# Decoder layer with attention, state-space scan and top-8 experts on one core: router sends split over the start of the expert stage, the last row's tail on other PSUM banks, and every queue's order written anew

## The chip, the core and the metric

One core of a Trainium2 chip runs one program. TensorE (PE in the profile, PEld for its weight loads) multiplies into PSUM banks; VectorE (DVE), ScalarE (ACT) and GpSimd (POOL) work element by element; SyncE (SP) only issues DMAs. POOL issues the indirect DMAs (gather and scatter by index). Each engine takes its instructions strictly in the order of its queue and waits at semaphores for the others. The metric is the device time of one execution in microseconds (us).

## The reference

```python
x = x + attn(layernorm(x))              # 4 rows of 512 tokens x 512; 16 heads of 128, one shared k and v
x = x + scan(ctx, layernorm(x))         # conv, 16 states: h = h * exp(dt*A) + dt*u*B ; y = sum(h*C)
x = x + moe(layernorm(x))               # 32 experts, the 8 best of each token, inner size 192
# moe: topv, topi = top_k(softmax(x @ gate.T), 8); weights under TAU are dropped, the rest renormed
```

## The kernel before

The four rows (index `b`, in the code also `r`) go one after the other, and a row's attention overlaps its scan and the end of the row before. The order of each engine's queue is written out call by call in the functions `first_row`, `row` (used three times) and `last_row`, once in each engine's block: SP from line 399, PE from 738, ACT from 1414, DVE from 2261, POOL from 2786.

**Start of row 0.** SP loads `Wq` (4 MB, into the tile `o_t`, line 366). `split_wq(g)` makes a high part of a quarter of it on ACT (line 1325) and a low part on DVE (line 2030), four quarters in `SPLIT_ORDER`. `first_stats`, `first_means`, `first_newton`, `first_norm` (lines 1969 to 1980) make the layer norm of x on DVE; `norm_tr` (PE, line 532) transposes it; `norm_hi`/`norm_lo` split the result. `scan_in` (PE, line 559) and `convolution` (DVE, lines 2021 and 2024, two pairs) feed the scan, `scan_u` (ACT) closes it, `scan_params` (line 585) and `step_size` (line 596) make its step. `keys_values`, `q_piece` (lines 573 to 575, 615 to 617), `key_squares`, `squares`, `q_scaled` (ACT) and `q_tr` lead to the first `scores`. `step_exp` and `step_log` (ACT, lines 1287 and 1294) belong to the scan's step.

**Scan.** For each of 16 states ACT makes `decays`, DVE `state_input`, two `state_scan` halves (line 2103) and `state_product`, and POOL adds the product to `y` by an accumulating DMA (`add_state`, line 2772). SP loads the b and c rows (`load_bc`, line 357).

**End of a row.** `out_proj(b, h)` (line 694) adds head h over four banks; it needs `load_wout(b, h)`, issued by SP in a written order among the `load_bc` (line 344). Then DVE: `last_sum`, `out_stats`, `out_means`, `out_gain`, `out_add`, `gate_stats`, `gated`, `add_scan`, `final_stats`, `final_norm`. The last row has no row behind it to overlap with. In it `proj_copy` (ACT) copies the projection from PSUM to SBUF ahead of `out_stats`; `out_tr` transposes the normed rows in four pieces, `out_copy` (ACT, line 1362) copies each to SBUF, `logits` (line 725) multiplies all four with the gate, and the router follows on DVE: `softmax_top`, `active`, then `ranks` on PE (lines 731 to 734), `slots` and `weights` (lines 2239 to 2244).

**Sends.** `send(t, k, ...)` scatters 128 tokens' entries to the list of the experts that they chose (line 2757): for each tile t of 128 tokens and each k, the k-th of a token's eight experts in ascending order of the expert. So the list of expert e is complete when the sends with k up to e have landed. A row has 32. Those of rows 0 to 2 are issued during the row behind (`send_some`); the 32 of row 3 stand at the head of the expert stage (`send_last`), four for each k.

**Expert stage.** 68 blocks of 128 tokens, two at least for each expert, in groups of four (`QUAD`). SP waits for the sends of expert e and loads the block's list (`get_ids`, lines 482 to 486); POOL gathers the tokens (`get`, line 2862); PE transposes, multiplies (lines 1145 and on), ACT weighs the result into `y_ring` (line 1894), and POOL adds it to the output by a scatter (`add`, line 2868). `get_next(q, r)` issues the gather for the block six further on. Before, POOL's order is: sends k = 0, 1; gets 0, 1; sends k = 2; gets 2, 3; sends k = 3; gets 4, 5; gets 6, 7; adds 0, 1; sends k = 4; gets 8, 9; adds 2, 3; sends k = 5; gets 10, 11; adds 4, 5; sends k = 6; gets 12, 13; adds 6, 7; sends k = 7; gets 14, 15; adds 8, 9; and from there gets and adds alone. Each get waits for the list that SP loads after the sends have landed.

## Time and profile before

| | us |
|---|---|
| median of 3 runs | 1616.96 |
| their range | 1614.8 to 1628.02 |
| the profiled execution | 1621.45 |
| its span on the core | 1619.7 |

PE is busy 86% of the span, DVE 69%, ACT 58%, POOL 30%. The mean granted clock of TensorE is 0.936 of full speed. In the 40 slices of the span PE is at 9 tenths nearly throughout, except in the first three slices, in slices 28 to 31 (about 1134 to 1296 us: the last row's tail and the start of the expert stage), where it shows 4, 3, 6, 5, and in the neighbours of these. Rows 0 to 3 take some 1145 us, the tail and the router 70, and the expert stage 405.

### The profile page before, as it was taken

The page shows a single profiled execution, that of the slowest core. Times are in us where ns is not written, and L with a number is a line of the kernel's source. Part 1 is how long each engine was busy: PE and PEld are TensorE (multiplying, and loading weights), DVE is VectorE, ACT ScalarE, POOL GpSimd, SP SyncE. Part 2 cuts the span into 40 slices and gives each one's busy share as a digit, 9 for nine tenths or more (in the row PEclk, how much of TensorE's full clock was granted, in tenths as well). Part 3 has the DMA queues.
Part 4 walks back from the last instruction along what each step waited for, and adds up shares of the span by engine and source line. Part 5 has one row for each costly group of instructions (what it writes and reads, how often), then busy time and mean ns, then how long its engine had stood idle before and what let it go on. Part 6 is the DMA issues. An engine that isn't in the chain of part 4 may idle for free.

```text
span 1619.7 us, 26021 instructions
## 1 busy us (share of the span) xinstructions
PE 1394.1 (86%) x6762; PEld 999.7 (62%) x6763; DVE 1110.4 (69%) x1547; ACT 944.5 (58%) x2428; POOL 486.6 (30%) x367
## 2 busy tenths in 40 slices
PE   4899898999999899999899999898436548999996
PEld 1577665548887455887644678763225436777774
DVE  5365598858898786878886887786853326666662
ACT  4667684468878246877725687763213325666652
POOL 0000010000143502006250210206426446666663
PEclk9799999999999999999999999999757779999998
DMA  6538987623679742576973267578124449999985
GB/s 240 201 109 223 292 204 178 151 93 81 182 193 227 179 107 80 126 230 138 226 175 94 61 173 208 116 175 250 41 87 104 102 98 222 223 238 231 243 185 67
DMA packets 137435, 265.44 MB, mean 164 GB/s; under 512 B 45944, under 2 KB 47433, under 8 KB 128512
## 3 DMA queue, kind: packets, MB, share of 16 engines
q0 software_dynamic: 36480, 126.75, 35.0%
q1 hardware_dynamic: 75120, 86.70, 18.5%
q10 hardware_dynamic: 25744, 50.87, 10.0%
...
## 4 chain that ended last, share of the span: by engine, by line
PE 50%; DMA 18%; issue 10%; DVE 9%; ACT 5%; SPq 3%; POOL 2%; POOLq 1%; ACTq 1%; DVEq 0%
PE bank L694 13%; PE bank L671 8%; DMA out<-y_ring,add_ids 4%; PE bank L654 4%; DMA y<-state 4%; PE pair L615 3%; PE pair L616 3%; PE pair L617 3%; DMA wout<-in_wout 2%; PE bank L532 2%; DMA c_bc<-bc_dram 2%; DMA y<-dbu 2%; PE pair L532 2%; PE pair L559 2%; DVE dbu L2103 1%
## 5 line engine op out<-in xcount | busy, mean ns | idle before, releaser
L694 PE MATMUL bank<-wout,o_t 128*128 128x512 f32 x512 | 241.0, 627 | 27.4 <-DMA wout<-in_wout 16.3
L671 PE MATMUL bank<-v_aug,probs 128*128 128x129 f32 x2048 | 249.1, 277 | 10.1 <-ACT probs L1331 7.1
L671 PEld LDWEIGHTS bank<-v_aug,probs 128*128 128x128 f32 x2048 | 240.5, 192 | 27.4 <-ACT probs L1331 19.9
L2757 POOL DMA_INDIRECT lists<-entry,slot x128 | 197.6, 1543 | 83.4 <-DVE entry L2244 44.7
L694 PEld LDWEIGHTS bank<-wout,o_t 128*128 128x128 f32 x512 | 101.2, 201 | 154.8 <-issue 154.3
L1331 ACT ACTIVATE probs<-bank 128x512 f32<-128x512 f32 x256 | 152.2, 604 | 69.0 <-PE bank L654 31.8
L1340 ACT ACTIVATE decay<-delta,neg_a 128x511 f32<-128x511 f32 x256 | 164.4, 725 | 24.4 <-DVE state L2103 12.1
L2868 POOL DMA_INDIRECT out<-y_ring,add_ids x68 | 125.0, 1838 | 96.6 <-DMA out<-y_ring,add_ids 52.3
L2772 POOL DMA_DIRECT2D y<-dbu x32 | 29.2, 913 | 412.6 <-DVE dbu L2108 254.0
L2103 DVE TENSOR_TENSOR_SCAN state<-decay,state 128x1024 f32<-128x1024 f32 x64 | 144.8, 2281 | 6.5 <-ACT decay L1340 4.7
L2103 DVE TENSOR_TENSOR_SCAN dbu<-decay,dbu 128x1024 f32<-128x1024 f32 x64 | 144.7, 2279 | 5.1 <-ACT decay L1340 4.2
L654 PE MATMUL bank<-q_t,k_t 128*128 128x512 f32 x256 | 126.8, 607 | 1.7 <-ACT q_t L1320 1.4
L615 PE MATMUL pair<-wq,xn_hi 128*128 128x512 f32 x256 | 110.2, 431 | 2.2 <-ACT q_s L1310 2.0
L2753 POOL DMA_DIRECT2D wq<-wq_dram x30 | 22.0, 765 | 300.1 <-PE pair L617 226.3
L1145 PE MATMUL bank<-w_hi,xt_hi 128*128 x272 | 99.9, 367 | 9.7 <-DVE xt_lo L2697 8.0
L1348 ACT ACTIVATE o_s<-bank,den 128x128 f32<-128x128 f32 x256 | 80.1, 373 | 46.4 <-DVE den L2121 41.1
...
L2862 POOL DMA_INDIRECT x_blk<-xf_dram,get_ids x70 | 85.2, 1218 | 60.9 <-DMA get_ids<-lists 31.8
L616 PE MATMUL pair<-wq,xn_hi 128*128 128x512 f32 x256 | 101.8, 398 | 0.0
L617 PE MATMUL pair<-wq,xn_lo 128*128 128x512 f32 x256 | 101.6, 397 | 0.0
L1881 ACT ACTIVATE xt_hi<-pair (+1 forms) x70 | 41.9, 598 | 102.1 <-PE pair L532 95.0
...
## 6 DMA issues: line engine op xcount, KB each, us to landing
...
```

The costliest lines, as they stand in the source:

```text
L615: pe.matmul(bank_q[t % 2][:], xn_hi[:, k, tile], wq[:, 0, k, :], start=(k == 0), stop=False)
L616: pe.matmul(bank_q[t % 2][:], xn_hi[:, k, tile], wq[:, 1, k, :], start=False, stop=False)
L617: mm = pe.matmul(bank_q[t % 2][:], xn_lo[:, k, tile], wq[:, 0, k, :], start=False, stop=(k == KT - 1))
L654: mm = pe.matmul(bank_s[k % 2][:], k_t[:, tile], q_t[:, j, :], start=True, stop=True)
L671: mm = pe.matmul(bank_o[half][:, (t % 2) * (DH + 1):(t % 2 + 1) * (DH + 1)], probs[:, k, t * P:(t + 1) * P], v_aug[:, k, :], start=(k == 0 ...
L694: mm = pe.matmul((bank_o + bank_s)[t][:], o_t[:, h, t * P:(t + 1) * P], wout[:, h % 4, :], start=(h == 0), stop=(h == H - 1))
L1145: pe.matmul(gu_bank[:, 0:2 * INTER], xt_hi[:, parity, k, :], hi[:, k, :], start=(k == 0), stop=False)
L1331: act.activation(probs[:, k, :], bank_s[k % 2][:], ACT.Exp).then_inc(S["exp_ok"], 1)
L1340: act.activation(dA3[:, e, 1:], delta[:, e, 1:], ACT.Exp, scale=neg_a[:, bass.ds(n, 1), e:e + 1].rearrange("p a c -> p (a c)")).then_inc(S ...
L2103: dve.tensor_tensor_scan(now, dA3[:, es, :].rearrange("p e t -> p (e t)"), now, 0.0, ALU.mult, ALU.add).then_inc(S["scan_ok"], 1)
L2757: pool.indirect_dma_start(out=lists, out_offset=bass.IndirectOffsetOnAxis(ap=slot[:, t, k:k + 1].bitcast(U32), axis=0), in_=entry[:, t, :] ...
L2868: pool.indirect_dma_start(out=out, out_offset=bass.IndirectOffsetOnAxis(ap=add_ids[:, r:r + 1].bitcast(U32), axis=0), in_=y_ring[:, r, :], ...
```

## The change

There are three parts.

1. **Sends of row 3.** POOL's new order is: sends k = 0, 1, 2; gets 0, 1; sends k = 3; gets 2, 3; sends k = 4; gets 4, 5; sends k = 5; gets 6, 7; adds 0, 1; sends k = 6; gets 8, 9; adds 2, 3; sends k = 7; gets 10, 11; adds 4, 5; and from there gets and adds alone. Each get of block pair e then stands behind sends up to k = e + 2.
2. **Tail of the last row.** `proj_copy` is gone there: `out_stats` and `out_gain` read the PSUM banks of the projection. The transposes of the scan's y use `bank_q`, those of the normed rows four banks of their own with no wait. `out_copy` is shared, ACT k = 0 and 2, DVE k = 1 and 3, and the gate's product is made piece by piece (`logit_part`). `weights` stands ahead of `slots`, `tokens` ahead of `gate_norm`, and the loads of experts 0 to 3 stand later in ACT's queue.
3. **Orders.** In all rows the calls on SP, PE, ACT, DVE and POOL are in a new order. In row 0, DVE begins with `split_wq` of the first quarter, ahead of `first_stats`, and has three quarters of it ahead of the second `convolution`; ACT has `split_wkv` and two `split_wq` ahead of `first_seed`, and `step_exp`, `step_log` ahead of `q_seed`, which it takes after `key_squares` and two `squares`.

The diff, cut: row 0's start on PE, ACT and DVE, the tail, SP's and POOL's last row, and the sends. The rows between are reordered in the same manner.

```diff
...
-y_banks = lambda b: bank_s if b == NB - 1 else bank_t[0:1]
-f_banks = lambda b: bank_o if b == NB - 1 else bank_t[0:1]
+y_banks = lambda b: bank_q if b == NB - 1 else bank_t[0:1]
+f_banks = lambda b: bank_o + bank_t if b == NB - 1 else bank_t[0:1]
...
-    if k >= len(banks):
-        pe.wait_ge(S["fT_ok"], b * KT + (k + 1 - len(banks)))
+    if b < NB - 1 and k > 0:
+        pe.wait_ge(S["fT_ok"], b * KT + k)
...
+def logit_part(b, k):
+    if k % 2 == 0:
+        pe.wait_ge(S["fT_ok"], b * KT + k // 2 + 1)
+    else:
+        pe.wait_ge(S["fTd_ok"], k // 2 + 1)
+    for t in range(TT):
+        mm = pe.matmul(bank_s[0][:, t * NE:(t + 1) * NE], end_s[:, k, t * P:(t + 1) * P], w_gate[:, k, :], start=(k == 0 and t == 0),
+                       stop=(k == KT - 1 and t == TT - 1))
+    if k == KT - 1:
+        mm.then_inc(S["lg_ps"], 1)
...
     scan_in(0, 2)
+    norm_tr(0, 0)
     scan_in(0, 3)
-    norm_tr(0, 0)
     norm_tr(0, 1)
+    norm_tr(0, 2)
     scan_params(0)
-    norm_tr(0, 2)
     norm_tr(0, 3)
     step_size(0, 0)
+    keys_values(0, 0)
     step_size(0, 1)
-    keys_values(0, 0)
+    keys_values(0, 1)
     step_size(0, 2)
+    keys_values(0, 2)
     step_size(0, 3)
-    keys_values(0, 1)
-    keys_values(0, 2)
     q_piece(0, 0, 0)
+    q_piece(0, 0, 1)
     keys_values(0, 3)
-    q_piece(0, 0, 1)
...
     neg_rates()
+    scan_pad(0, 0)
+    split_wkv()
+    split_wq(SPLIT_ORDER[0])
+    split_wq(SPLIT_ORDER[1])
+    scan_pad(0, 1)
     first_seed(0)
-    scan_pad(0, 0)
-    scan_pad(0, 1)
     scan_pad(0, 2)
-    split_wkv()
+    norm_hi(0, 0)
+    split_wq(SPLIT_ORDER[2])
     scan_pad(0, 3)
+    norm_hi(0, 1)
     scan_u(0)
-    norm_hi(0, 0)
-    norm_hi(0, 1)
-    split_wq(SPLIT_ORDER[0])
+    scan_rows(0)
     norm_hi(0, 2)
     norm_hi(0, 3)
-    scan_rows(0)
-    split_wq(SPLIT_ORDER[1])
     step_parts(0, 0)
     step_parts(0, 1)
-    split_wq(SPLIT_ORDER[2])
+    split_wq(SPLIT_ORDER[3])
     step_parts(0, 2)
     step_parts(0, 3)
     value_copy(0, 0)
-    step_exp(0)
-    step_log(0)
     key_squares(0)
-    value_copy(0, 1)
     squares(0, 0, 0)
     squares(0, 0, 1)
+    step_exp(0)
     q_seed(0, "q0")
+    step_log(0)
...
-    load_expert(0)
     divide(b, 15, 1)
     split_expert(0, 0)
-    load_expert(1)
+    decays(b, 11)
+    head_copy(b, 14)
     decays(b, 12)
-    split_expert(0, 1)
-    head_copy(b, 14)
-    split_expert(1, 0)
-    head_copy(b, 15)
     decays(b, 13)
     decays(b, 14)
-    load_expert(2)
+    load_expert(1)
+    split_expert(0, 1)
+    split_expert(1, 0)
     decays(b, 15)
-    proj_copy(b, 0)
-    proj_copy(b, 1)
-    proj_copy(b, 2)
-    proj_copy(b, 3)
+    head_copy(b, 15)
     norm_seed(b, "o")
     norm_seed(b, "z")
     gates(b)
+    load_expert(2)
     norm_seed(b, "f")
+    load_expert(3)
+    out_copy(b, 0)
     split_expert(1, 1)
+    out_copy(b, 2)
+    logit_exps(b)
     split_expert(2, 0)
-    out_copy(b, 0)
-    out_copy(b, 1)
-    out_copy(b, 2)
-    out_copy(b, 3)
     split_expert(2, 1)
-    logit_exps(b)
-    load_expert(3)
...
+def proj_out(b, t):
+    return (bank_o + bank_s)[t][:] if b == NB - 1 else o_c[:, t, :]
 def out_stats(b, t):
-    dve.wait_ge(S["oc_ok"], b * TT + t + 1)
-    stats(b, "o", o_c[:, t, :], t)
+    if b == NB - 1:
+        dve.wait_ge(S["op_ps"], b * TT + t + 1)
+    else:
+        dve.wait_ge(S["oc_ok"], b * TT + t + 1)
+    stats(b, "o", proj_out(b, t), t)
...
-    dve.tensor_tensor(x_sb[:, t, :], x_sb[:, t, :], (bank_s[t % 2] if b == NB - 1 else bank_t[0])[:], ALU.add).then_inc(S["x2_ok"], 1)
+    dve.tensor_tensor(x_sb[:, t, :], x_sb[:, t, :], (bank_q[t % 2] if b == NB - 1 else bank_t[0])[:], ALU.add).then_inc(S["x2_ok"], 1)
...
+def out_copy(b, k):
+    dve.wait_ge(S["fT_ps"], b * KT + k + 1)
+    dve.tensor_copy(end_s[:, k, :], (bank_o + bank_t)[k][:]).then_inc(S["fTd_ok"], 1)
...
 def first_row():
+    split_wq(SPLIT_ORDER[0])
     first_stats(0, 0)
     first_stats(0, 1)
     dve.wait_ge(S["w_in_sb"], 16 * N_W)
...
     first_norm(0, 0)
     first_norm(0, 1)
     convolution(0, 0)
-    convolution(0, 1)
     first_norm(0, 2)
+    split_wq(SPLIT_ORDER[1])
     first_norm(0, 3)
+    split_wkv()
     norm_lo(0, 0)
     norm_lo(0, 1)
-    split_wkv()
-    split_wq(SPLIT_ORDER[0])
+    split_wq(SPLIT_ORDER[2])
+    convolution(0, 1)
     norm_lo(0, 2)
     norm_lo(0, 3)
-    split_wq(SPLIT_ORDER[1])
-    split_wq(SPLIT_ORDER[2])
+    softplus(0)
     q_norm(0, "k")
     q_norm(0, "q0")
     keys(0, 0)
+    softplus_rest(0)
+    split_wq(SPLIT_ORDER[3])
     keys(0, 1)
-    split_wq(SPLIT_ORDER[3])
+    key_lo(0)
     q_norm(0, "q1")
-    softplus(0)
-    key_lo(0)
-    softplus_rest(0)
+    softplus_log(0)
+    denominators(0, 0, 0)
+    denominators(0, 0, 1)
+    denominators(0, 1, 0)
+    q_lows(0, 0, 2)
+    softplus_sum(0)
+    scan_du(0)
     wq_stored(dve)
     skip(0)
-    q_lows(0, 0, 2)
...
...
     load_bc(b, 9)
     load_bc(b, 10)
     load_bc(b, 11)
+    load_wout(b, 4)
+    load_wout(b, 5)
     load_bc(b, 12)
-    load_wout(b, 5)
-    load_wout(b, 4)
+    load_wout(b, 7)
     load_wout(b, 6)
     load_bc(b, 13)
-    load_wout(b, 7)
     load_wout(b, 8)
+    load_wout(b, 10)
+    load_bc(b, 14)
     load_wout(b, 9)
-    load_bc(b, 14)
+    load_wout(b, 11)
+    load_bc(b, 15)
+    load_wout(b, 14)
     load_wout(b, 12)
-    load_wout(b, 10)
-    load_bc(b, 15)
     load_wout(b, 13)
-    load_wout(b, 11)
-    load_wout(b, 14)
     load_wout(b, 15)
...
     last_sum(b)
+    out_stats(b, 0)
     dve.wait_ge(S["oT_ok"], NB * H)
     split(0, 0)
-    out_stats(b, 0)
     out_stats(b, 1)
...
+    tokens(b)
     gate_norm(b)
     split(0, 1)
...
+    out_copy(b, 1)
+    out_copy(b, 3)
     split(1, 0)
     softmax_top(b)
     active(b)
+    weights(b)
     slots(b)
-    weights(b)
     split(1, 1)
...
 def last_row(b):
+    add_state(b, 5)
     send_some(b - 1, 0, 3)
-    add_state(b, 5)
     add_state(b, 6)
     send_some(b - 1, 3, 6)
+    send_some(b - 1, 6, 9)
     add_state(b, 7)
     add_state(b, 8)
     add_state(b, 9)
+    send_some(b - 1, 9, 12)
+    send_some(b - 1, 12, 15)
     add_state(b, 10)
     add_state(b, 11)
-    send_some(b - 1, 6, 9)
+    send_some(b - 1, 15, 18)
     add_state(b, 12)
-    send_some(b - 1, 9, 12)
-    send_some(b - 1, 12, 15)
     add_state(b, 13)
-    send_some(b - 1, 15, 18)
     send_some(b - 1, 18, 21)
     add_state(b, 14)
...
-send_last(range(0, 2))
+send_last(range(0, 3))
 pool.wait_ge(S["xf_out"], NB * 16)
 pool.wait_ge(S["blank_ok"], 1)
 pool.wait_ge(S["rows_ok"], 2)
-for r in range(2):
+for r in range(QUAD):
+    if r % MIN_BLK == 0 and r > 0:
+        send_last(range(r // MIN_BLK + 2, r // MIN_BLK + 3))
     pool.wait_ge(S[f"get_in{r}"], 32)
     get(r)
-send_last(range(2, 3))
-for r in range(2, QUAD):
-    pool.wait_ge(S[f"get_in{r}"], 32)
-    get(r)
-send_last(range(3, 4))
+send_last(range(4, 5))
 for r in range(2):
     get_next(-1, r + 2)
 last_quad = pool.value_load(tab[0:1, T_LAST:T_LAST + 1], min_val=NE * MIN_BLK // QUAD - 1, max_val=MAX_BLK // QUAD - 1)
 pool.wait_ge(S["x2_out"], NB * 16)
 for q in range(2):
     for r in range(0, QUAD, 2):
-        k = q * 2 + r // 2 + 3
-        if k in range(4, TOPK):
+        k = q * 2 + r // 2 + 5
+        if k < TOPK:
             send_last(range(k, k + 1))
         get_next(q, r)
         get_next(q, r + 1)
         add_pair(q, r)
-send_last(range(TOPK - 1, TOPK))
```

## Rows read from the trace of the kernel before

**Rows 1.** Windows: stretch, us, busy of PE PEld DVE ACT POOL, clock, DMA share, GB/s.
```profile
120.00:200.00 80.00, 71.14 (x398) 56.23 (x397) 42.33 (x37) 53.94 (x166) 5.03 (x6) 0.96 0.93 260
200.00:300.00 100.00, 88.31 (x433) 59.63 (x432) 85.23 (x72) 57.12 (x140) 9.06 (x11) 0.97 0.77 187
435.00:770.00 335.00, 321.29 (x1656) 232.16 (x1655) 272.57 (x368) 229.33 (x673) 105.65 (x76) 0.98 0.63 161
1215.00:1345.00 130.00, 77.78 (x345) 62.36 (x345) 44.19 (x86) 42.22 (x72) 66.60 (x53) 0.78 0.48 109
1345.00:1608.00 263.00, 241.96 (x1229) 190.10 (x1227) 164.71 (x317) 152.48 (x262) 166.76 (x108) 0.99 0.86 207
```
**Rows 2.** Timeline, ACT's weighed blocks 7 and 13: start, us, engine line op [idle before].
```profile
1292.41 0.69 ACT L1894 ACTIVATE y_ring<-bank,meta 128x512 f32 x1 [2.03 <-PE bank L1164]
1346.17 0.69 ACT L1894 ACTIVATE y_ring<-bank,meta 128x512 f32 x1 [0.96 <-PE bank L1164]
```
**Rows 3.** The line view of L1894: count, duration min/median/max in ns, first and last start.
```profile
L1894 ACT ACTIVATE y_ring<-bank,meta x68: 687/688/692, 1238.7 to 1607.8; 128x512 f32 x68
```
**Rows 4.** Timeline, POOL at the start of the expert stage.
```profile
1201.93 1.67 POOL L2757 DMA_INDIRECT lists<-entry,slot  x1 [44.71 <-DVE entry L2244]
...
1218.40 1.05 POOL L2862 DMA_INDIRECT x_blk<-xf_dram,get_ids  x1 [5.82 <-DMA get_ids<-lists]
...
1250.23 1.03 POOL L2757 DMA_INDIRECT lists<-entry,slot  x1 [0.31 <-issue]
...
1260.43 2.29 POOL L2862 DMA_INDIRECT x_blk<-xf_dram,get_ids  x1 [4.77 <-DMA get_ids<-lists]
...
1287.52 1.03 POOL L2862 DMA_INDIRECT x_blk<-xf_dram,get_ids  x1 [1.71 <-DMA get_ids<-lists]
1289.36 1.62 POOL L2868 DMA_INDIRECT out<-y_ring,add_ids  x1 [0.81 <-issue]
...
1328.02 1.05 POOL L2862 DMA_INDIRECT x_blk<-xf_dram,get_ids  x1 [7.61 <-issue]
```
**Rows 5.** DMA issues: out<-in, queue, KB each, median us from issue to landing.
```profile
o_t<-in_wq SPq DMA_DIRECT2D x1, 4096.0 KB, 14.5
```
**Rows 6.** Timeline, start of row 0, in order of time, all engines.
```profile
11.77 0.51 SPq L366 DMA_DIRECT2D o_t<-in_wq  x1
14.85 1.29 DVE L1969 BATCH_NORM_STATS2 st<-q_s 128x6 f32<-128x512 f32 x2
20.96 4.06 DVE L2024 SCALAR_TENSOR_TENSOR dbu<-decay,conv_w,dbu 128x512 f32<-128x512 f32 x6
30.75 1.97 PE L532 MATMUL pair<-const,probs 128*128 128x128 f32 x8 [7.49 <-DVE probs L1980]
32.65 4.61 PE L585 MATMUL bank<-state,w_x 128*48 128x512 f32 x8
33.34 1.90 ACT L1325 ACTIVATE du<-o_t 128x2048 fp32r<-128x2048 f32 x1
35.28 2.29 DVE L2030 TENSOR_TENSOR o_t<-o_t,du 128x2048 fp32r<-128x2048 f32 x1
40.16 2.46 PE L596 MATMUL pair<-x_dbl,w_dt 16*128 16x512 f32 x4 [1.88 <-DVE xn_lo L2039]
77.28 1.97 PE L532 MATMUL pair<-const,q_s 128*128 128x128 f32 x8 [4.56 <-ACT q_s L1310]
```
**Rows 7.** Timeline, the last row's projection and closing sum.
```profile
1126.03 22.97 PE L694 MATMUL bank<-wout,o_t 128*128 128x512 f32 x48 [5.51 <-DMA wout<-in_wout]
1146.21 2.29 DVE L2115 TENSOR_TENSOR o_t<-y,state 128x2048 f32<-128x2048 f32 x1 [2.28 <-PE bank L694]
```
**Rows 8.** Timeline, the tail: transposes, gate product, first instruction of `weights`.
```profile
1177.22 3.90 PE L532 MATMUL bank<-const,xf 128*128 128x128 f32 x16 [5.80 <-DVE xf L1980]
1181.86 4.27 PE L725 MATMUL bank<-w_gate,o_t 128*128 128x32 f32 x32 [0.75 <-ACT o_t L1362]
...
1199.72 0.29 DVE L2239 TENSOR_TENSOR o_t<-o_t 128x128 f32<-128x128 f32 x1
```

614 lines of the change are left out of this document (305 added, 309 removed).

## The prediction

> **What bounds the kernel now.** I read the page first, then windows over each stage, then the timelines of the places that the diff touches. The windows show three regimes. In the rows PE sets the pace: in 335 us of the middle it is busy 321.3 and idle 13.7, with DVE at 272.6 [rows 1]. The late blocks of the expert stage are bound by PE as well (242 of 263 us) [rows 1]. Between them lies a stretch, 1215 to 1345 us, where PE is busy 78 of 130 us and DVE and ACT a third of the time [rows 1]. There POOL's queue sets the pace. The weighed blocks show it: the first is at 1238.7, block 13 at 1346.17, the last (67) at 1607.8 [rows 2, 3]. So the first 13 take 107.5 us, 8.3 each, and the other 54 take 261.6 us, 4.84 each. At the start, row 0 isn't bound by PE: it waits for norms, conversions and the scan's step.
>
> **Sends (part 1).** Before, the gets of blocks 8 and 14 start at 1260.43 and 1328.02 [rows 4]: three pairs in 67.6 us, 22.5 a pair. In each pair the queue is four sends (from 1250.23 to 1260.43 less the idle of 4.77, so to 1255.66: 5.4; up to 0.8 more where one is slow), then the wait until these sends have landed and SP has loaded the list from them (4.77 and, three pairs on, 7.61), the gets with another wait of about 2 between them (1.71 in the row), and two adds of 1.6 each with gaps of 0.3 to 0.8 [rows 4]. PE follows the gather four blocks ahead: block 7 is weighed at 1292.41, 4.9 after the get of block 11 at 1287.52 [rows 2, 4].
>
> After, a get finds its sends two pairs old, so both waits go. A pair is then 5.6 of sends, 2.75 of two gets, 3.8 of two adds and 0.9 of gaps, some 13. The four more sends ahead of get 0 cost nothing: eight sends run from 1201.93 at about 1.29 each to 1212.6, the next four end at 1217.9, and get 0 starts at 1218.40 since it waits 5.82 for its list [rows 4]. The adds of blocks 0 and 1 ended just before 1250.23 [rows 4]. After, sends k = 4 and 5 stand ahead of them besides; that is eight sends more than before, of which four fit in the gap of 5.8 and one is offset by other short waits in that stretch: +4 x 1.29 less these, so this point comes at some 1252 (1255 without the offset, within the bounds below). From there: sends k = 6 to 1257.6; get 8 at 1259.7, with 2 us kept for blocks whose result is late; gets and adds and sends k = 7, get 10 at 1272.6; get 11 at 1275.3, so block 7 at 1275.3 + 4.9 = 1280.2. No send is left behind it, and six blocks at PE's own 4.84 put block 13 at 1309.2, against 1346.17: **-37** for the likely case. Bounds: with pairs of 11 to 12 us (no slow send) the gain is 41. From above, if each of the first pairs keeps one wait of 4.77, two pairs lose 9.5, and the pace of 4.84 begins one pair later (6 us lost at most against it): -37 + 9.5 + 4 = about -24.
>
> **Tail (part 2).** The transposes of the normed rows start at 1177.22 and the gate product ends at 1186.13, with four copies on ACT between [rows 8]. Four banks and copies on two engines close the gap of 0.75 and let the pieces of the product (4.27 in all) run behind each copy; but PE's own work, 3.90 + 4.27, stays, of 8.91 in all: -0.7 to -1, I take -1.0. `weights` (five small instructions, from 1199.72 [rows 8], sends from 1201.93 [rows 4]: 1.4 us of DVE) goes under the ranks, which PE makes while DVE waits: -1.4. `tokens` now waits for row 2's sends ahead of `gate_norm`; POOL's last one ended 44.71 before 1201.93, at 1157.2 [rows 4], and the new place comes at about 1161, so the wait is covered by 3 to 4 us; without that cover it would cost at most those. Sum: **-2.4**, from 0 to -4. The removed `proj_copy` is worth nothing by itself: `last_sum` (1146.21, 2.29) runs on DVE at the same time [rows 7], and DVE makes the same four statistics behind it, now from PSUM. If a read from PSUM made each of the eight `out_stats` and `out_gain` 0.1 us longer, that would be +0.8; I keep it in the range and not in the sum.
>
> **End of the last row (part 3).** PE stalls 5.51 us ahead of 1126.03 for a `wout` load [rows 7]: The written order issues head 12's ahead of head 10's. The new order has 10 ahead of 14 and 12, and each load but one stands at or ahead of its old place. The stall would go, -5.5; but some of the time is taken by the closing sum, which waits for the scan's last add, with POOL's sends in front. I take **-5**, from -8 to 0.
>
> **Rows 0 to 2 (part 3).** The same amount of work in another order, on PE, which idles only 14 us in 335 [rows 1]. All of that gone would be -14 in each row, one more stall like that of the last row 5.5 and a colder clock behind it. Neither can be read from a queue order, so I take **0**, and keep +23 (a stall of 7.6 in each) as a rival.
>
> **Start of row 0 (part 3), against the change.** `Wq` is issued at 11.77 [rows 6] and takes 14.5 us to land [rows 5]: 26.3. Before, DVE starts its statistics at 14.85 and has both convolutions done by 29.7, in the shadow of this load; PE has the first norm transpose at 30.75, the scan's product at 32.65, `step_size` at 40.16 and the first `q_tr` at 77.28 [rows 6]. After, the first thing in DVE's queue is the low part of a quarter of `Wq`, which waits for the load and for ACT's high part (1.90): 26.3 + 1.9 + 2.29 = 30.5 [rows 5, 6]. Only then statistics (2.6 for four tiles), aggregation and the seed from ACT (some 2), two norms (1.0), the first convolution (4.06 + 0.9 for its first products), a norm, a quarter of `Wq` (2.2), a norm: the first norms are transposed at about 44 instead of 30.75. The second convolution stands behind two `norm_lo`, `split_wkv` (1.2) and a third quarter (2.3): done at about 58. Then `scan_u`, `scan_params` (4.61) and the first `step_size` at about 65.8 instead of 40.16: +25.6. ACT adds `step_exp` and `step_log` ahead of the seed for q; each works on 128x2048 like the conversions (1.90), but needs all four `step_size`; and `key_squares` waits for all keys. That makes another 3.8 and the four `step_size` between keys: the first `q_tr` comes at about 111 instead of 77.28, **+33**. Of this PE can give back what it idles later in the row: 80.0 - 71.1 and 100.0 - 88.3 [rows 1], 8.9 + 11.7 = 20.6. So the front is +13 at least, and +39 if ACT's extra pieces line up badly. I take +33, since the scan on DVE starts as late as the heads and its chain then lies on the end of the row.
>
> The Trainium skill speaks against it as well: "DMA: Bandwidth & Descriptors", section "Rules for kernel authors", says to issue a DMA early, do compute, and wait on its semaphore late; here DVE waits first and computes behind it. Its section "Anatomy of one DMA — SWDGE (gpsimd) path" gives about 2.0 us and bytes over 436 GB/s, that is an estimate of 11.6 us for 4 MiB where the row has 14.5 [rows 5]; by it the front would cost 2.9 less.
>
> **Sum.** -37 - 2.4 - 5 + 0 + 33 = -11.4. The profiled execution took 1621.45 (span 1619.7), 4.5 above the median of 1616.96; so 1610.0 for it, and 1605.5 as the median.
>
> **The rivals.**
> - *The front is absorbed.* PE and DVE fill their idle time in row 0 and take back 20: 1605.5 - 20 = 1585.5. For it: the idle time is there, and the heads don't depend on the scan until the row's end. Against: that idle time has its own reasons (DMA share 0.93 in 120 to 200 [rows 1]). Chance 0.26.
> - *Slower.* The new orders of SP put a `wout` load behind b and c loads in each of rows 0 to 2, and PE stalls 5.5 and runs colder for 2.1 in each: +22.8, and the last row keeps its 5: 1605.5 + 22.8 + 5 = about 1633. It decides from one and a half stalls a row on. Against: the middle rows' orders differ by a few places only. Chance 0.12.
> - *A new wait on the sends' way.* The adds, the gathers and the loads of lists crowd, and pairs stay near 18 us: -24 instead of -37, 1605.5 + 13 = 1618.5. For it: a single get waited 7.61 for a list though one pair before 4.77 sufficed [rows 4]. Chance 0.14.
> - The forecast: 1605.5, its own range 1596 to 1614. Chance 0.48.
>
> **How the numbers follow.** A measurement of this kernel tells 1% (16 us) from no change: faster is below 1600.8, slower above 1633.1. Faster is the first rival and a fifth of the forecast's case: 0.36. Slower: the second, 0.12. Same: the rest, 0.52. The range for 8 in 10 goes from 1580 (below it a third of the absorbed case) to 1630 (above it the slow one).
>
> **What would show it.** Right: the first norm transpose on PE near 44 and the first `q_tr` near 111; no waits of 4 us or more for lists ahead of gets 8 to 15, and block 13 weighed some 70 us behind the first block instead of 107.5; no gap of 5 us in the last row's projection. Wrong: a row 0 whose PE idle behind the late start is well under 20 us (the first rival); a PE idle in rows 0 to 2 well over 14 us in 335 (the second); pairs of gets still 18 us or more apart (the third).

## The result, and the profile after

| | before | after |
|---|---|---|
| median of 20 runs | 1617.2 | 1623.45 |
| lowest | 1604.65 | 1618.88 |
| ratio after/before, 95% interval | | 1.0046 (1.0025 to 1.0067) |
| span of the profiled execution | 1619.7 | 1623.6 |

The change is 0.46% slower, about 7 us. Forecast was 11 us faster. One of the 20 executions after took 2371.56 us, at a mean granted clock of 0.553, and is left out of the ratio. The time lies within the range and within 1% of before, but on the other side.

In the following table both traces are cut at the same places, from the start of one kind of instruction to the next. It accounts for 2.7 of the 3.9 us between the two spans; the other 1.2 lie behind block 67.

| stretch | before | after | difference | forecast |
|---|---|---|---|---|
| start to the first exps of row 0 | 81.3 | 117.5 | +36.2 | +33 |
| first exps of row 0 to those of row 1 | 281.7 | 290.3 | +8.6 | 0 |
| row 1 to row 2 | 273.5 | 279.9 | +6.4 | 0 |
| row 2 to row 3 | 275.3 | 277.6 | +2.3 | 0 |
| row 3, first to last exps | 167.9 | 162.1 | -5.8 | -5, with the next |
| last exps to the end of the projection | 69.3 | 73.3 | +4.0 | |
| end of the projection to the first send of row 3 | 52.9 | 47.1 | -5.9 | -2.4 |
| first send to block 0 weighed | 36.7 | 34.2 | -2.5 | 0 |
| block 0 to block 13 | 107.5 | 74.6 | -33.0 | -37 |
| block 13 to block 67 | 261.6 | 254.0 | -7.6 | 0 |
| sum | | | +2.7 | -11.4 |

The forecast's two large terms are there. Three rows behind them were forecast at 0 and cost 17.

**Expert stage.** Windows of the kernel after: stretch, us, busy of PE PEld DVE ACT POOL, clock, DMA share, GB/s. They answer to [rows 1]:

```profile
120.00:200.00 80.00, 71.28 (x391) 56.00 (x391) 46.78 (x45) 52.77 (x165) 4.12 (x5) 0.97 0.43 110
200.00:300.00 100.00, 92.09 (x546) 72.65 (x545) 77.06 (x70) 74.03 (x214) 9.37 (x12) 0.97 0.96 261
...
1260.00:1345.00 85.00, 61.63 (x296) 49.41 (x297) 36.31 (x72) 35.78 (x61) 59.92 (x50) 0.85 0.59 136
1345.00:1610.00 265.00, 249.51 (x1277) 197.57 (x1276) 171.99 (x331) 158.73 (x272) 171.24 (x111) 1.00 0.89 215
```

These windows (one left out, 435 to 770 us) don't hold the same blocks as those of [rows 1]: before, block 13 is weighed at the end of the stretch from 1215 to 1345, and here 11 us behind its end. From the first get to block 13, the same work in both kernels (first line before, second after):

```profile
1218.40:1346.20 127.80, 78.97 (x350) 63.09 (x351) 44.91 (x87) 42.46 (x73) 67.67 (x53) 0.78 0.49 114
1265.10:1356.50 91.40, 72.31 (x349) 57.33 (x349) 44.56 (x87) 42.47 (x73) 65.81 (x51) 0.89 0.66 155
```

It takes 91.4 us instead of 127.8, and PE is busy 79% of it instead of 62%. Of the 36 us, 6.7 are PE's busy time itself: it does the same work at a mean granted clock of 0.89 instead of 0.78. The last stretch is denser too: PE is busy 94% of it where it was 92%. The blocks, by the timeline and the line view of ACT's y_ring (they answer to [rows 2, 3]):

```profile
1328.75 0.69 ACT L1903 ACTIVATE y_ring<-bank,meta 128x512 f32 x1 [2.03 <-PE bank L1179]
1356.46 0.69 ACT L1903 ACTIVATE y_ring<-bank,meta 128x512 f32 x1 [0.99 <-PE bank L1179]
L1903 ACT ACTIVATE y_ring<-bank,meta x68: 687/688/691, 1281.9 to 1610.5; 128x512 f32 x68
```

Blocks 0, 7, 13 and 67 are weighed at 1281.9, 1328.75, 1356.46 and 1610.5. POOL's timeline shows the pairs (they answer to [rows 4]); the gets are L2884, sends L2779, adds L2890:

```profile
1265.11 1.05 POOL L2884 DMA_INDIRECT x_blk<-xf_dram,get_ids  x1 [0.80 <-issue]
...
1303.29 1.05 POOL L2884 DMA_INDIRECT x_blk<-xf_dram,get_ids  x1 [0.31 <-issue]
...
1305.98 2.20 POOL L2890 DMA_INDIRECT out<-y_ring,add_ids  x1 [0.30 <-issue]
1312.59 1.56 POOL L2890 DMA_INDIRECT out<-y_ring,add_ids  x1 [4.41 <-DMA out<-y_ring,add_ids]
...
1321.32 1.06 POOL L2884 DMA_INDIRECT x_blk<-xf_dram,get_ids  x1 [0.30 <-issue]
...
1327.82 1.08 POOL L2884 DMA_INDIRECT x_blk<-xf_dram,get_ids  x1 [0.30 <-issue]
```

No get waits more than 0.82 us for its list any more: get 8 at 1303.29 stands 0.31 behind its predecessor, where it had waited 4.77 [rows 4]. Gets 8, 10 and 12 come 18.0 and 6.5 us apart. In the first of these gaps one add waits 4.41 for an earlier add; up to get 12 this is the one wait of over 1 us that is left. One pair, 8 to 10, is thus as slow as the prediction's third rival had it.

POOL's waits (line waited for: us in total, times, longest), before from 1200 to 1345 us and then after from 1240 to 1350:

```profile
POOL x_blk L2862 <- DMA get_ids<-lists: 31.8, 8, 7.9
```

```profile
POOL x_blk L2884 <- DMA get_ids<-lists: 1.1, 2, 0.8
```

**Start of row 0.** Timeline of the kernel after, in order of time (it answers to [rows 6]):

```profile
25.91 1.91 ACT L1340 ACTIVATE du<-o_t 128x2048 fp32r<-128x2048 f32 x1 [5.97 <-DMA o_t<-in_wq]
27.93 2.29 DVE L2039 TENSOR_TENSOR o_t<-o_t,du 128x2048 fp32r<-128x2048 f32 x1 [26.94 <-ACT du L1340]
30.13 1.28 DVE L1978 BATCH_NORM_STATS2 st<-q_s 128x6 f32<-128x512 f32 x2
43.19 1.12 PE L532 MATMUL pair<-const,probs 128*128 128x128 f32 x4 [21.21 <-DVE probs L1989]
52.81 4.06 DVE L2033 SCALAR_TENSOR_TENSOR dbu<-decay,conv_w,dbu 128x512 f32<-128x512 f32 x6
66.75 2.04 PE L596 MATMUL pair<-x_dbl,w_dt 16*128 16x512 f32 x2 [2.20 <-DVE xn_lo L2048]
113.47 1.12 PE L532 MATMUL pair<-const,q_s 128*128 128x128 f32 x4 [5.53 <-ACT q_s L1325]
```

DVE waits 26.94 us for ACT's first half, which waits for `Wq`. The statistics start at 30.13; before, the first two of the four tiles stood at 6.30, ahead of the 14.85 that the prediction reads as their start [rows 6], and the other two at 14.85. Behind them the first norm transpose comes at 43.19 instead of 30.75, the first `step_size` at 66.75 instead of 40.16, the first `q_tr` at 113.47 instead of 77.28.

**Last row and tail.** Timeline of PE in the kernel after (it answers to [rows 7, 8]):

```profile
1156.18 10.54 PE L694 MATMUL bank<-wout,o_t 128*128 128x512 f32 x24 [2.46 <-DMA wout<-in_wout]
1169.71 13.56 PE L694 MATMUL bank<-wout,o_t 128*128 128x512 f32 x24 [2.99 <-DMA wout<-in_wout]
1183.80 3.67 PE L694 MATMUL bank<-wout,o_t 128*128 128x512 f32 x8 [0.52 <-DMA wout<-in_wout]
1189.65 3.67 PE L694 MATMUL bank<-wout,o_t 128*128 128x512 f32 x8 [2.18 <-DMA wout<-in_wout]
...
1226.82 3.67 PE L532 MATMUL bank<-const,xf 128*128 128x128 f32 x16 [6.15 <-DVE xf L1989]
1230.29 3.76 PE L735 MATMUL bank<-w_gate,o_t 128*128 128x32 f32 x32
```

The stall of 5.51 in one piece became four of 2.46, 2.99, 0.52 and 2.18, 8.15 in all. In the tail the gap between transposes and gate product is gone, and both together take 7.2 us instead of 8.9.

**Rows 1 to 3.** PE's waits from 270 to 1160 us: the kernel before (with its stall of 5.5 in the last projection), then after (with the first of the four above).

```profile
PE bank L694 <- DMA wout<-in_wout: 16.3, 7, 5.5
PE bank L694 <- issue: 8.3, 3, 3.5
```

```profile
PE pair L532 <- DVE probs L1989: 16.1, 3, 6.0
PE bank L694 <- DMA wout<-in_wout: 13.5, 4, 3.8
PE bank L694 <- issue: 4.2, 4, 1.1
```

A wait that wasn't there stands first: three times some 5.4 us, once in each row, PE's `norm_tr` waits for DVE's `first_norm` (line 1989). `norm_tr(r, 0)` waits for all four of them (line 540), so for the last. The middle one of the three, first DVE, then PE:

```profile
584.41 2.29 DVE L2104 TENSOR_TENSOR dbu<-du,b_bc 128x2048 f32<-128x2048 f32 x1 [5.31 <-DMA c_bc<-bc_dram]
...
592.77 2.28 DVE L2112 TENSOR_TENSOR_SCAN dbu<-decay,dbu 128x1024 f32<-128x1024 f32 x1
594.97 0.52 DVE L1989 TENSOR_SCALAR probs<-q_s,mv,rs_n 128x512 f32<-128x512 f32 x1
...
595.55 1.12 PE L532 MATMUL pair<-const,probs 128*128 128x128 f32 x4 [4.84 <-DVE probs L1989]
```

DVE itself stands still for 5.31 us ahead of `state_input` 12 (line 2104), which comes before all four norms, for that state's b and c rows. In the three rows DVE waits 5.66, 5.31 and 6.49 us there, and PE 5.20, 4.84 and 6.03. In the kernel before DVE has no such wait, and the fourth norm is done 4.6, 4.1 and 3.1 us before PE comes for it.

The three rows as a whole, from the first exps of row 0 to those of row 3 (windows; before, then after):

```profile
81.30:911.80 830.50, 782.33 (x3809) 542.80 (x3808) 633.11 (x735) 539.46 (x1541) 170.20 (x133) 0.97 0.63 163
117.50:965.30 847.80, 791.52 (x3821) 545.97 (x3821) 631.02 (x740) 536.80 (x1543) 173.84 (x133) 0.96 0.61 158
```

Of the 17.3 us only 8.1 are idle time of PE (56.3 instead of 48.2; other waits have shrunk beside the new 16.1). The other 9.2 are busy time: the granted clock is 0.96 instead of 0.97, and 12 more matmuls fall into the stretch, nearly all of them in row 0. Seven are missing from row 3's heads in exchange (964 instead of 971), so part of the +8.6 and of the -5.8 in the first table is work that has changed its stretch.

### The profile page after: what moved, and what is told of

It reads as the page before. It is cut to its first block, busy times and chain, and to the rows that moved or that the text cites. A ratio compares the mean times of both kernels' runs of the same rounds, so it can differ in the third digit from the quotient of the medians.

```text
span 1623.6 us, 26011 instructions
## 1 busy us (share of the span) xinstructions
PE 1393.9 (86%) x6762; PEld 993.7 (61%) x6763; DVE 1108.8 (68%) x1549; ACT 936.9 (58%) x2422; POOL 493.5 (30%) x367
## 4 chain that ended last, share of the span: by engine, by line
PE 42%; DMA 27%; DVE 12%; issue 10%; ACT 5%; POOL 2%; SPq 2%; POOLq 1%; DVEq 0%; ACTq 0%
DMA out<-y_ring,add_ids 14%; PE bank L671 10%; PE bank L694 7%; PE bank L654 5%; DMA y<-state 3%; DMA wout<-in_wout 3%; DMA y<-dbu 3%; PE pair L615 2%; PE pair L617 2%; PE pair L616 2%; DMA c_bc<-bc_dram 2%; PE bank L532 2%; PE pair L532 2%; DVE dbu L2033 1%; DVE state L2117 1%
## 5 line engine op out<-in xcount | busy, mean ns | idle before, releaser
L694 PE MATMUL bank<-wout,o_t 128*128 128x512 f32 x512 | 248.1, 641 | 23.5 <-DMA wout<-in_wout 19.2
L671 PEld LDWEIGHTS bank<-v_aug,probs 128*128 128x128 f32 x2048 | 239.8, 192 | 23.9 <-ACT probs L1346 18.4
L2779 POOL DMA_INDIRECT lists<-entry,slot x128 | 205.1, 1603 | 100.3 <-DVE slot L2275 61.2
L2890 POOL DMA_INDIRECT out<-y_ring,add_ids x68 | 125.1, 1840 | 92.2 <-DMA out<-y_ring,add_ids 71.1
L615 PE MATMUL pair<-wq,xn_hi 128*128 128x512 f32 x256 | 110.9, 433 | 15.6 <-ACT q_s L1325 10.9
L2104 DVE TENSOR_TENSOR dbu<-du,b_bc 128x2048 f32<-128x2048 f32 x32 | 73.2, 2289 | 41.6 <-DMA c_bc<-bc_dram 26.9
L1363 ACT ACTIVATE o_s<-bank,den 128x128 f32<-128x128 f32 x256 | 80.7, 380 | 34.5 <-DVE den L2130 27.4
L1161 PE MATMUL bank<-w_lo,xt_hi 128*128 x272 | 92.6, 340 | 0.0
L1162 PE MATMUL bank<-w_hi,xt_lo 128*128 x272 | 92.3, 340 | 0.0
```

The costliest lines, as they stand in the source:

```text
L615: pe.matmul(bank_q[t % 2][:], xn_hi[:, k, tile], wq[:, 0, k, :], start=(k == 0), stop=False)
L671: mm = pe.matmul(bank_o[half][:, (t % 2) * (DH + 1):(t % 2 + 1) * (DH + 1)], probs[:, k, t * P:(t + 1) * P], v_aug[:, k, :], start=(k == 0 ...
L694: mm = pe.matmul((bank_o + bank_s)[t][:], o_t[:, h, t * P:(t + 1) * P], wout[:, h % 4, :], start=(h == 0), stop=(h == H - 1))
L2779: pool.indirect_dma_start(out=lists, out_offset=bass.IndirectOffsetOnAxis(ap=slot[:, t, k:k + 1].bitcast(U32), axis=0), in_=entry[:, t, :] ...
L2890: pool.indirect_dma_start(out=out, out_offset=bass.IndirectOffsetOnAxis(ap=add_ids[:, r:r + 1].bitcast(U32), axis=0), in_=y_ring[:, r, :], ...
```

## The experiments

Each ratio is to the kernel before, timed beside it. The medians of that kernel went from 1612.74 to 1621.17 in these four sets, so the ratios are compared and not the medians. "Changed" is the kernel after. The five kernels for the start of row 0 have one execution each; for those the trace is read.

### The large terms: front_old, sends_only, old_orders, rows_old

Whole functions are exchanged between the two kernels.

```diff
 # front_old = changed, but on all five queues:
-first_row() of after
+first_row() of before
 # rows_old = changed, but on all five queues:
-row(b, r) of after
+row(b, r) of before
 # sends_only = before, and on POOL behind last_row:
-send_last(range(0, 2)) ... send_last(range(TOPK - 1, TOPK))   # before
+send_last(range(0, 3)) ... k = q * 2 + r // 2 + 5             # after
 # old_orders = changed with first_row and row of before, and last_row of before up to last_sum,
 #              then the new tail
```

> The changed kernel with the first_row of the kernel before on all five queues. My theory (the late start of row 0 costs 36 us and nothing gives it back): the first exps at 81 instead of 117.5, all behind it earlier by 36, so 1623.5 - 36 = 1587, ratio to the kernel before 0.982. Rival (row 0 and the rows behind absorb most of it): less than 15 us, 1608 or more, ratio over 0.994.

> The kernel before with only the new order of row 3's sends. My theory (POOL's sends and the waits for lists pace the first 13 blocks): block 13 weighed some 70 to 75 us behind the first one instead of 107.5, and the whole kernel 33 to 40 us faster, 1577 to 1584, ratio 0.976 to 0.980. Rival (much of the gain in the changed kernel comes from the tail or from where the loads of experts stand): under 25 us, ratio over 0.985.

> The kernel before with the new sends and the new tail behind last_sum, and every queue's old order up to there. My theory (the new orders are where the gain goes): sends -33 to -40, tail -2 to -8, so -35 to -48: 1569 to 1582, ratio 0.970 to 0.978. Rival (the tail needs the new order of the last row): no better than the sends alone.

> The changed kernel with the row function of the kernel before on all five queues, so rows 0 to 2 behind their start. From single traces the scores of row 1 lag by 37 us and those of row 3 by 45. Theory 1 (the new order of the rows costs these 8 us): 1615.5, ratio to the kernel before 0.999. Theory 2 (the 8 us are scatter from run to run): 1623.5, ratio 1.004.

| | median | ratio to before (95%) |
|---|---|---|
| front_old | 1582.31 | 0.978 (0.972 to 0.984) |
| sends_only | 1578.97 | 0.976 (0.970 to 0.982) |
| old_orders | 1574.98 | 0.977 (0.970 to 0.983) |
| rows_old | 1610.87 | 0.996 (0.993 to 1.000) |

*front_old*: the start of row 0 costs the changed kernel its 36 us in the end as well (1.0046 - 0.978, 2.7%, 43 us with an uncertainty of 10). Nothing behind gives it back. *sends_only*: the sends are worth 2.4% by themselves. Its blocks 0, 13 and 67 are weighed 72.5 and 252.5 us apart. *old_orders*: with the new tail besides, 0.977, it is no better than the sends alone, as the rival had it, but two ratios with 0.6% of uncertainty each can't show the tail; tail_only below does. *rows_old*: the new order of the rows costs; with the old one the changed kernel is 0.8% (13 us, with an uncertainty of 7) faster. In its trace the rows from exps to exps take 283.7, 273.5 and 274.0 instead of 290.3, 279.9 and 277.6. So it wasn't scatter.

### Where row 0 loses: seed_early, conv_pair, seed_conv, seed_conv_exp, seed_conv_keys

All are edits of the changed kernel's first_row; the later ones contain the earlier.

```diff
 # seed_early; DVE:
-split_wq(SPLIT_ORDER[0])        # first in the queue
...
 convolution(0, 0)
+split_wq(SPLIT_ORDER[0])
 # ACT: first_seed(0) behind neg_rates(), scan_pad(0, 1) behind scan_pad(0, 0)
 # conv_pair; DVE: convolution(0, 1) right behind convolution(0, 0); ACT: scan_pad(0, 2), (0, 3), scan_u(0)
 #            ahead of norm_hi(0, 0); PE: norm_tr(0, 0) behind scan_in(0, 3)
 # seed_conv = both
 # seed_conv_exp; ACT:
+step_exp(0)
+step_log(0)
 key_squares(0)
...
-step_exp(0)
 q_seed(0, "q0")
-step_log(0)
 # seed_conv_keys; PE: step_size(0, 0), (0, 1), keys_values(0, 0), step_size(0, 2), (0, 3),
 #                 keys_values(0, 1), (0, 2), q_piece(0, 0, 0), keys_values(0, 3), q_piece(0, 0, 1)
```

> The changed kernel; in row 0 alone, DVE's low part of the first quarter of Wq moved from the head of its queue to behind the first convolution, and ACT's first_seed and second scan_pad ahead of its two conversions. Theory 1 (the wait for Wq at the head of two queues is the main cause of the 36 us): the first norm transpose on PE at about 31 instead of 43.2 and the first exps 25 to 33 us earlier, 85 to 92. Theory 2 (mine: two delays of like size in series, the wait for Wq and the second convolution behind three conversions): norm transpose at 31, but the first exps only about 11 us earlier, 106.

> The changed kernel; in row 0 alone, the second convolution right behind the first on DVE, with scan_pad, scan_u and scan_in moved forward on ACT and PE so that it can. Theory 1: the first exps hardly earlier, under 5 us. Theory 2: the first step_size at about 55 instead of 66.8, the first exps about 11 us earlier, 106.

> Both edits of row 0 together. Theory 2: step_size near 43, and the first exps at about 92, that is 25 us earlier than in the changed kernel; the 10 us that stay against the 81.3 of the kernel before are those of step_exp, step_log and key_squares on ACT. If it is still over 100, a third delay in the new order of row 0 is larger than I hold it to be.

> The two edits of row 0 (seed_conv) and, besides, ACT's step_exp and step_log ahead of key_squares, where ACT idles 6.5 us for the last keys. The third delay by my theory: these two (1.90 each) and DVE's softplus behind them hold up the q norms by 5 us. Expected: first exps at 91 to 92 instead of 96.0. Rival (the late fourth keys_values holds everything up): 96.

> seed_conv_exp with, besides, PE's order of step_size, keys_values and q_piece at the start of row 0 as before: four step_size nearly together, and the last keys_values ahead of the second q_piece. Theory 1 (PE's interleaving of these is the third delay): the first exps at 87 to 89 instead of 96.3. Rival (the order of ACT and DVE behind them keeps it): 94 to 96.

Measured, each in one trace:

| | first norm_tr | first step_size | first q_tr | first exps | time |
|---|---|---|---|---|---|
| before | 30.75 | 40.16 | 77.28 | 81.3 | |
| after | 43.19 | 66.75 | 113.47 | 117.5 | |
| seed_early | 33.88 | 57.67 | 106.90 | 110.9 | 1617.73 |
| conv_pair | 49.22 | 61.68 | 104.24 | 108.3 | 1615.84 |
| seed_conv | 34.88 | 46.56 | 91.97 | 96.0 | 1601.13 |
| seed_conv_exp | 35.40 | 47.22 | 92.26 | 96.3 | 1596.53 |
| seed_conv_keys | 35.61 | 47.62 | 85.79 | 89.8 | 1596.96 |

Theory 1 of seed_early fell: with the wait for `Wq` out of the way the first exps come only 6.6 us earlier. The convolution alone gives 9.2, both 21.5. Theory 2 had 11, 11 and 25. Simple delays in series would give 15.8 together; 5.7 come only when both are gone, so each alone is partly hidden behind the other (conv_pair's first `norm_tr` even comes 6.0 later than after). The single values carry some scatter: over all traces with the whole new start the first exps stand at 117.5 to 122.7, over those with the whole old one at 75.1 to 83.2. seed_conv_exp changed nothing, so my reason for the third delay was wrong. The trace of seed_conv_exp showed another: PE's four `step_size` stand apart by a `keys_values` each, and the last `keys_values` behind two `q_piece`. ACT's key_squares waits for it, and q waits for ACT:

```profile
72.03 0.28 ACT L1281 ACTIVATE junk<-bank 128x128 bf16<-128x128 f32 x1 [4.09 <-PE bank L575]
78.02 0.76 PE L615 MATMUL pair<-wq,xn_hi 128*128 128x512 f32 x1 [6.03 <-ACT q_s L1325]
```

The first is ACT, idle 4.09 until the last `keys_values` (line 575), the second PE, idle 6.03 until ACT has scaled q. With PE's old order (seed_conv_keys) the first `q_piece` of the second pair starts at 71.36 instead of 78.02, and the exps at 89.8, 6.5 us earlier:

```profile
71.36 0.77 PE L615 MATMUL pair<-wq,xn_hi 128*128 128x512 f32 x1 [3.63 <-ACT q_s L1325]
```

The gap is larger than scatter where it arises: from the first `step_size` to the first `q_tr` it is 38.2 us instead of 45.0. Its one execution doesn't show these 6.5 (1596.96 beside 1596.53), but the kernel before had a median of 1621.17 beside the one and of 1612.74 beside the other. Whether they last to the end was not settled. Some 8 us of the 36 are left in orders that weren't tried one by one.

### Why the rows are longer: norm_tr_late, norms_early, sp_rows_old

```diff
 # norm_tr_late; PE, row:
-norm_tr(r, 0)
 out_proj(b, 4)
-norm_tr(r, 1)
-norm_tr(r, 2)
 out_proj(b, 5)
+norm_tr(r, 0)
+norm_tr(r, 1)
+norm_tr(r, 2)
 norm_tr(r, 3)
 # norms_early; DVE, row:
 first_means(r)
+first_newton(r)
 state_scan(b, 11, 1)
+first_norm(r, 0)
+first_norm(r, 1)
 state_input(b, 12)
 state_product(b, 11)
-first_newton(r)
 state_scan(b, 12, 0)
-first_norm(r, 0)
-first_norm(r, 1)
 # sp_rows_old = changed with row of before on SP alone
```

> The changed kernel; in the rows, PE's four norm_tr of the next row moved behind out_proj(b, 5), nothing else. The trace of the changed kernel shows PE idle 16.1 us in three stays before norm_tr, waiting for DVE's first_norm. Theory 1 (this wait is what makes the new rows slower): -10 to -16 us, 1608 to 1613, ratio to the kernel before 0.994 to 0.998. Theory 2 (the wait moves on to the next product, which waits for a wout load or for the same norms): under 4 us, ratio 1.002 or more.

> The changed kernel; in the rows, DVE's first_newton and the first two first_norm moved ahead of state_input 12, state_product 11 and the first half of state_scan 12 (6.9 us of DVE), as in the kernel before; nothing else. Theory 1 (DVE's late norms make the new rows 4.4 us longer each, 278.7 instead of 274.3): the wait of 5.4 before norm_tr goes without coming back, 8 to 13 us faster than the changed kernel, 1610 to 1615, ratio to the kernel before 0.996 to 0.999. Theory 2 (PE's later waits, for wout and for norm_lo, take its place, as when norm_tr was moved): under 4 us, ratio 1.002 or more.

> The changed kernel with SP's order of the rows as before, every other queue new. Theory 1 (the order of the wout loads among the b and c loads is what makes the rows longer): 8 to 13 us faster than the changed kernel, ratio 0.996 to 0.999. Theory 2 (it is the order on DVE and PE): 0, ratio 1.004, and rows of 278 us as in the changed kernel.

| | median | ratio to before (95%) | rows, exps to exps |
|---|---|---|---|
| after | 1623.45 | 1.0046 (1.0025 to 1.0067) | 290.3, 279.9, 277.6 |
| norm_tr_late | 1623.39 | 1.0047 (1.0023 to 1.0071) | 291.4, 279.0, 278.1 |
| norms_early | 1610.58 | 0.9988 (0.9964 to 1.0012) | 288.0, 273.2, 273.6 |
| sp_rows_old | 1646.08 | 1.0214 (1.0168 to 1.0259) | 294.5, 283.2, 277.4 |

PE's waits of each over the same stretch, 270 to 1160 us; first norm_tr_late:

```profile
PE bank L694 <- DMA wout<-in_wout: 23.2, 4, 7.3
PE pair L532 <- DVE xn_lo L2048: 10.8, 6, 2.4
```

norms_early:

```profile
PE pair L532 <- DVE probs L1989: 13.2, 3, 5.0
PE bank L694 <- DMA wout<-in_wout: 7.9, 3, 3.6
```

sp_rows_old:

```profile
PE bank L694 <- DMA wout<-in_wout: 20.1, 4, 8.9
PE bank L694 <- issue: 7.7, 4, 2.8
```

With `norm_tr` moved behind more work, its wait of 16.1 is gone, but 10.8 come back at the next wait for a norm and 9.7 more at the `wout` loads. The rows are as long as before that edit. With two of the four norms moved on DVE, the producer of the wait, rows 1 and 2 come down to 273.4 (row 0 stays at 288.0), and the time by 0.6% (9 us, with an uncertainty of 5). The trace shows how: the wait for the norms shrinks by 2.9 only, that for `wout` by 5.6, and PE's busy time from exps to exps by 6.9 (784.60 instead of 791.52, at a granted clock of 0.97 instead of 0.96). So it isn't the one wait that was shortened, but the queue behind it: a late product `out_proj` also gives back its `wout` buffer late, and the next load starts late. That this link is the reason for the 5.6 is read from the order of events and wasn't tested alone.

Why the wait itself hardly shrinks: the third and the fourth norm stay behind `state_input` 12, and DVE still waits 4.75, 2.88 and 4.41 us there for the b and c rows, PE 5.05, 3.32 and 4.86 for the fourth norm. By SP's queue that load goes out late. First the changed kernel, then the kernel before (`q_t<-in_ctx_t` is the first load of `next_ctx`, `b_bc` and `c_bc` that of state 12):

```profile
570.68 0.38 SPq L311 DMA_DIRECT2D q_t<-in_ctx_t  x1
...
572.07 1.45 SPq L357 DMA_DIRECT2D b_bc<-bc_dram  x1
573.56 1.22 SPq L357 DMA_DIRECT2D c_bc<-bc_dram  x1
```

```profile
524.27 0.32 SPq L357 DMA_DIRECT2D b_bc<-bc_dram  x1
524.63 0.51 SPq L357 DMA_DIRECT2D c_bc<-bc_dram  x1
...
548.87 0.38 SPq L311 DMA_DIRECT2D q_t<-in_ctx_t  x1
```

The new order puts `next_ctx`, with its wait for the row's last scores, ahead of `load_bc(b, 12)`, where it stood behind `load_bc(b, 13)`. The load is issued 7 us before DVE is ready for it instead of 16, its c row lands 10.8 us after its issue where the median of these loads is 5.3, and DVE starts at 584.41. No run moves `next_ctx` alone. sp_rows_old takes it back with all of SP's order, and there DVE waits for state 12's load no more and PE's wait for the norms is 5.0 instead of 16.1; but both of its theories fell, since the loads in the old order under products in the new one cost 27 us (with an uncertainty of 8) more than the changed kernel. Its trace is only 14.1 us longer than that of the changed kernel, 7.4 of it in rows 0 to 2 and 5.2 in the heads of row 3, so half of that price isn't located.

### The last row and the tail: last_old, last_rows_new, tail_only

```diff
 # last_old = changed with last_row of before on all queues, up to last_sum (the tail stays new)
 # last_rows_new = old_orders with last_row of after
 # tail_only = old_orders with the sends of before
```

> The changed kernel with the last row's orders of before on all queues, up to the tail, which stays new. My forecast held the new last row to be worth -5; four traces since give it 0, with a scatter of 6. Theory 1 (worth 0): 1623.5, ratio 1.004. Theory 2 (worth the -5 of the forecast): 1628, ratio 1.007. Theory 3 (the new orders cost, as in the rows): 1618, ratio 1.001.

> The changed kernel with first_row and row of before, that is old_orders with the last row's orders new. Theory 1 (the new last row is worth the forecast's -5 to -8, as last_old showed behind the new rows): 1567 to 1570, ratio 0.970 to 0.973. Theory 2 (last_old's loss came of the seam between the new rows and the old last row): 1575, ratio 0.976.

> The kernel before with only the new tail of the last row, behind last_sum; old sends, old orders. The forecast gave the tail -2.4. Traces with the new tail show its sends 4 to 6 us earlier after the projection than before, and old_orders stands 4.0 below sends_only. Theory 1 (tail worth 4 to 6): 1609 to 1611 beside a before of 1615, ratio 0.996 to 0.9975. Theory 2 (2.4, as forecast): ratio 0.9985.

| | median | ratio to before (95%) | row 3, first to last exps |
|---|---|---|---|
| last_old | 1631.26 | 1.0110 (1.0068 to 1.0152) | 167.1 |
| last_rows_new | 1565.38 | 0.9690 (0.9638 to 0.9742) | 162.6 |
| tail_only | 1609.93 | 0.9955 (0.9922 to 0.9988) | 168.0 |

The new last row is worth 0.6% (10 us, with an uncertainty of 8) behind the new rows, and 0.8% (12 us, from two sets, with an uncertainty of 13, so not clear of 0) behind the old ones. The stretch that differs is the heads: 162.0 to 163.2 us from the first to the last exps in twelve of the thirteen traces that have it, 167.1 to 168.0 in the traces with the old one (before, sends_only, tail_only, old_orders, last_old); the thirteenth, sp_rows_old, has 167.3 with SP's loads of the rows in the old order. With the same rows ahead and the same 964 matmuls, PE is idle 2.5 us there in the changed kernel and 6.7 in last_old. From the last exps to the end of the projection the traces scatter from 68.4 to 79.0 with the new one and from 69.1 to 72.0 with the old one, and the two stretches together from 230.4 to 242.1 and from 236.7 to 239.8. Of last_old's three theories only the second holds, of last_rows_new's the first. The tail is worth 0.45% (7 us, from 2 to 13), as theory 1 of tail_only has it, but theory 2 lies within the interval too.

### The two costs taken out: front_norms

```diff
 # front_norms = changed with first_row of before on all queues, and norms_early's edit on DVE
```

> The changed kernel with both costs taken out: first_row of before, and in the rows first_newton and two first_norm early as in norms_early. If the two causes are separate and together all that the new orders cost, their gains add: 1623.5 - 41 - 12.5 = 1570, ratio 0.971 to 0.974, as good as last_rows_new. If they overlap: 1580, ratio 0.978.

Measured 1569.23, ratio 0.9701 (0.9656 to 0.9747). The two gains add: 2.7% and 0.6% make 3.3%, and front_norms is 3.45% under the changed kernel. It is level with last_rows_new (0.969). Both are 3% faster than the kernel before and 3.5% faster than the changed one. They share the sends, the tail, the new last row and the old start.

## Why the prediction was wrong

*Start of row 0: right.* Each step of the chain came within 3 us: first statistics behind 30.5 (30.13), norm transpose 44 (43.19), `step_size` 65.8 (66.75), `q_tr` 111 (113.47). The rule of the Trainium skill that was set against the change ("DMA: Bandwidth & Descriptors", section "Rules for kernel authors": issue early, compute, wait late) held in its direction, but seed_early shows that the early wait makes only 6.6 of the 36. The other page figure, 11.6 us for the load, is not what the trace shows: ACT starts at 25.91, 14.2 us behind the issue at 11.67 (the page gives it for the GpSimd path, and this load goes out from SP). For the last part of the chain, from `step_size` to `q_tr` (46.7 us instead of 37.1), I had named `step_exp` and `step_log`; that reason was wrong, and PE's interleaving of `step_size` and `keys_values` holds most of it, 6.9. The sum was right with a wrong part in it, and that the parts came out so close is in part luck.

*Absorbed by row 0: didn't happen.* The idle time of PE at 120 to 300 us was 20.6 and is 16.6 now; the rival had a chance of 0.26.

*Sends: right.* Forecast -37 to block 13. Counted from the first send, block 13 is weighed after 108.8 us instead of 144.2, -35.5; 2.5 of it fall before block 0, where I had nothing. Get 8 starts 38.2 behind get 0 where I had 41.3, get 10 56.2 where I had 54.2, since an add waits 4.41. What I had not counted is behind block 13: from there to block 67 it takes 7.6 us less, although no send stands there in either kernel but k = 7 at its edge; 3.7 of the 7.6 fall before block 20. sends_only shows 2.4%, 38 us, of which the account of its trace gives 35.0 up to block 13 and 9.1 behind. The part behind block 13 scatters, though: with the old sends it is 261.6 us (before) and 257.1 (tail_only), with the new ones 252.5 to 256.7. The prediction also took the 7.61 ahead of get 14 for a wait for a list, where the row says "issue"; the wait for a list of that size is the 7.86 ahead of get 12.

*Tail: right, and a part beside it.* -2.4 forecast. The pieces that I had priced at -1.0 and -1.4 came as -1.7 (transposes and gate product, 7.2 for 8.9) and -2.2 (from there to the first send, 13.6 for 15.8). The other 2.0 of the -5.9 lie ahead of the transposes. In all thirteen traces with the new last row DVE has `last_sum` done and starts its statistics 2.48 us before the end of the projection, and the transposes start 26.2 us behind that end instead of 28.2; with the old last row under the new tail they start at 27.4 to 28.2. So these 2.0 need both parts. In nine of the other traces with the new tail (front_old is one) it is 50.2 us from the end of the projection to the first send and not 47.1. Up to the gate's product they match the kernel after within 0.02 us, and this product makes the difference:

```profile
1185.07 6.88 PE L735 MATMUL bank<-w_gate,o_t 128*128 128x32 f32 x32
1181.88 7.03 PE L725 MATMUL bank<-w_gate,o_t 128*128 128x32 f32 x32 [0.75 <-ACT o_t L1362]
```

The first is front_old's, the second that of sends_only, which has the old tail: both at a granted clock of 0.50, the lower level (1.2 GHz), where the kernels before and after take 4.27 and 3.76. So like is compared with like: at the lower level throughout, 50.2 us (front_old) against 55.5 (sends_only), -5.3; in the kernels after and before, where the clock rises in between, 47.1 against 52.9, -5.9. tail_only has -3.4 without the new last row, and 7 us in its time, with an interval from 2 to 13.

*Last row: right in size, wrong in place.* -5 forecast. Its heads take 5.8 us less, and the timed kernels show 10. But the stall that I had named as the gain, 5.51, is 8.15 now, and the projection ends 4.0 later behind its heads. What pays is not the mechanism that I named, so that the size came out right is luck. Which part of the new last row shortens its heads wasn't tried.

*Rows 0 to 2: the step that failed.* I wrote that neither gain nor loss "can be read from a queue order, so I take 0". The term put at 0 measured 17 us in the trace and 13, with an uncertainty of 7, in rows_old. Much of it could be read. On PE the diff moves `head_tr(b, 15)`, and with it the wait for the last head, away from in front of `norm_tr(r, 0)`, so PE gets there earlier. On DVE it moves the first half of `state_scan` 12 (2.3 us) ahead of the first `first_norm`, so that is later. On SP it moves `next_ctx` ahead of state 12's load, so DVE waits 5.3 to 6.5 us ahead of all four norms. A consumer that moves forward and a producer that moves back make a wait. The load is the largest of the three parts: each time DVE's wait for it is 0.46 or 0.47 us longer than PE's wait for the norms, so by the traces the other two alone would have made no wait. That is argued from the traces; no run takes the load's part out by itself. (norms_early puts two norms ahead of 6.9 us of scan work, 4.6 more than the kernel before did; my expectation of it said "as in the kernel before", which is true of `first_newton` alone.) Nor is the wait the whole cost: more than half of the 17 us is PE's busy time, at a lower granted clock and with 12 more matmuls in row 0. The slower rival had a stall of 5.5 in each row, the right size, and a colder clock behind it, but at the `wout` loads and with a chance of 0.12. Of the 18 us between forecast and result in the median, this one term makes 13 to 17.
